# A decoder layer on one core: the work ahead of the loop over the tiles of heads in another order

## The chip, the core and the metric

The kernel runs on one core of a Trainium2 chip. A core has five engines, each with its own list of instructions and no scheduler between them: TensorE (PE) multiplies, with its weight loads shown apart (PEld), VectorE (DVE), ScalarE (ACT) and GpSimd (POOL) work on vectors, and SyncE (SP) issues the transfers. They wait for each other only where the program says so, with semaphores. The metric is the device time of one execution in microseconds (us). Before the change it is 1687.86 us, the median of 3 runs (1687.23 to 1689.83).

## The reference

One decoder layer over 8 sequences of 128 tokens, 512 features. Its first part is a Mamba-2 layer, and the change lies in the beginning of that part:

```python
proj = jnp.einsum('bsd,ed->bse', x, in_proj_w)
gate, hBC, dt = proj[..., :INTER], proj[..., INTER:INTER + CONV_DIM], proj[..., INTER + CONV_DIM:]
xc = conv_general_dilated(xc, conv_w, ...)           # 4 taps along the sequence, per channel
hBC = jax.nn.silu(xc + conv_b)                       # heads (8192 channels), B and C (8 groups of 128)
dt = jnp.clip(jax.nn.softplus(dt + dt_bias), 0.0, 100.0)
A_cum = jnp.cumsum(dt * -jnp.exp(A_log), axis=-1)    # along the sequence, 128 heads
L = jnp.exp(_segsum(A_dt))
Y_diag = jnp.einsum('bzlhn,bzshn,bhzls,bzshp->bzlhp', C, B, L, hs * dt)
g = (Y + hs * D) * jax.nn.silu(gate)                 # then a norm over each group, times out_proj_w
```

A cross attention and a gated feed-forward follow, with layer norms between; the change does not touch them.

## The kernel before

**Precision by splitting.** Every fp32 product of the projections is made of three products of rounded parts: x and the weights are split into a high part (a cast) and a low part (the difference), and `mm3` adds high x high, high x low and low x high. A projection of one tile of 128 channels over one half of the tokens (512) is 4 x 3 = 12 products of 128x512 into one PSUM bank.

**Steps.** The channels are walked in 72 steps (`STEPS`), 9 for each of 8 groups. The first step of a group projects its B (into `ps_hs`) and C (into `ps_gate`); the other 8 project one tile of heads (`heads`) and its gate (`gates`). TensorE works one step ahead: in step s it projects step s + 1, then turns and multiplies for step s. After a projection ScalarE writes the first tap with the bias (`first_tap`, into `conv`), VectorE adds the other three (`taps`, semaphore `tap`), ScalarE takes the SiLU (`silu`; `gate` for the gate's). A tile then goes: TensorE turns it to tokens (`transposes`), VectorE scales it by dt (`scale_dt`, which also frees the gate's bank), ScalarE takes four exponentials of the differences of cumulative sums (`decay`), VectorE multiplies each by the products of B and C kept in `cb`, and TensorE multiplies (`outputs`). VectorE's `taps` of the next step stand between its four decay products.

**Buffers for the weights.** `w_raw`, `w_hi` and `w_lo` have two slots, slot s % 2 for step s. GpSimd's `split(s)` makes both parts. It waits for the transfer and for the gate products of step s - 2, which read the same slot (`gate_ps` at 2s - 2).

**Cumulative sums.** dt of all heads is projected first of all into `ps_y` (weights in half of slot 1), goes through ScalarE and VectorE as softplus, is multiplied by -exp(A_log) and summed along each sequence by 8 scans. The sums go out to DRAM and come back broadcast to all partitions (`cum_load`, into `cum_bc`), where GpSimd masks what is not causal (`keep_causal`) and adds the negated sum of the other token (`differences`). TensorE turns dt and the sums to tokens (`turn_all`), and they are copied to `dt_tok` and, negated, to `neg_cum`. Both dt arrays and x share memory: `dt_v`, `dt_u`, `dt_w`, `dt_l` are the four parts of `x_raw`, named `g_acc` in the profile.

**Order.** Each engine's order is the order of the code in its block. Before the loop GpSimd makes the splits of steps 0 and 1 and both masks of tile 0; in the loop's first step it makes the split of step 2 and then both differences of tile 0. VectorE runs dt's whole chain with the scans ahead of the taps of B and C. The taps of one step are counted on one semaphore, 3 for each bank.

## Time and profile before

| what | before |
|---|---|
| time, median of 3 | 1687.86 us |
| the profiled execution's own time | 1687.67 us |
| its span | 1685.9 us |
| mean granted TensorE clock | 0.989 |
| TensorE busy | 1625.2 us, 96% of the span |
| VectorE, ScalarE, GpSimd busy | 1179.1, 948.9, 947.3 us |

The span is the time from the first to the last instruction that the profiler recorded. Busy times add up the recorded lengths; a product's recorded length holds its pipeline, so neighbouring products overlap and their pitch is less than their length. A granted clock of 1.00 is 2.4 GHz, one of 0.50 is 1.2 GHz. All rows of a timeline carry the start in us from the start of the span, the time, the engine, the line, what is written from what, and the count; a bracket names how long the engine was idle before and what ended that.

### The profile page before, as it was taken

The numbers are of one execution on the slowest core, as the hardware profiler recorded it, in microseconds if no ns is written. First come the engines' busy times: TensorE is split into PE (matmuls) and PEld (weight loads), VectorE is DVE, ScalarE is ACT, GpSimd is POOL, SyncE is SP. The second block draws the span as 40 slices with busy tenths as digits, with TensorE's granted clock in tenths as the row PEclk, the third lists the DMA queues.
The fourth block names the chain that finished last, engine by engine and source line by source line (L and its number), as shares of the span: only waits on it lengthen the run. The fifth ranks groups of instructions, "written<-read, shape, count | busy, mean of one in ns | idle before, by whom it ended". The sixth has DMA issues, their size and how long they took to land.

```text
span 1685.9 us, 25533 instructions
## 1 busy us (share of the span) xinstructions
PE 1625.2 (96%) x9160; PEld 1278.2 (76%) x9160; DVE 1179.1 (70%) x2257; ACT 948.9 (56%) x1577; POOL 947.3 (56%) x716
## 2 busy tenths in 40 slices
PE   6899999999999999999999999999999978889998
PEld 4788888888888888888888888888888865444646
DVE  4785858685868586858684868486848668896443
ACT  3583648364837383738373847384738354995231
POOL 3594839483949294929493949395929562231000
PEclk8999999999999999999999999999999989999999
DMA  5241224131423142313231323142314181001000
GB/s 206 71 136 58 99 66 135 63 101 59 135 70 101 57 132 76 101 57 132 76 100 57 132 71 105 52 135 62 115 45 137 63 139 57 1 11 29 13 13 25
DMA packets 76546, 138.84 MB, mean 82 GB/s; under 512 B 6786, under 2 KB 13954, under 8 KB 76164
## 3 DMA queue, kind: packets, MB, share of 16 engines
q1 hardware_dynamic: 76420, 137.21, 25.9%
q8 instruction: 73, 1.20, 0.3%
q14 instruction: 53, 0.43, 0.1%
HBM read 134.55 MB, written 2.63 MB: 81 GB/s over the span
## 4 chain that ended last, share of the span: by engine, by line
PE 90%; DVE 5%; ACT 2%; issue 1%; DMA 1%; SPq 1%; POOL 0%; DVEq 0%; ACTq 0%
PE ps_hs L246 8%; PE ps_hs L248 8%; PE ps_hs L247 8%; PE ps_gate L246 8%; PE ps_gate L248 8%; PE ps_gate L247 8%; PE ps_y L1123 7%; PE ps_hs L1131 7%; PE ps_hs L1133 7%; PE ps_hs L1132 7%; PE ps_gate L1112 4%; PE ps_y L1358 3%; PE ps_hs L1320 3%; PE ps_dec L1320 3%; DVE pr L959 1%
## 5 line engine op out<-in xcount | busy, mean ns | idle before, releaser
L750 DVE SCALAR_TENSOR_TENSOR conv<-ps_hs,cw,conv 128x508 f32<-128x508 f32 (+2 forms) x432 | 320.3, 742 | 30.7 <-ACT conv L511 19.6
L378 POOL TENSOR_SCALAR_AFFINE_SELECT cum_bc<-cum_bc 128x1024 f32<-128x1024 f32 x128 | 140.1, 1095 | 238.9 <-DMA cum_bc<-cum_scratch 238.2
L388 POOL TENSOR_TENSOR cum_bc<-cum_bc,neg_cum 128x1024 f32<-128x1024 f32 x128 | 247.7, 1936 | 23.1 <-DVE neg_cum L855 12.6
L246 PE MATMUL ps_hs<-x_hi,w_hi 128*128 128x512 f32 x576 | 232.6, 404 | 7.8 <-DVE conv L750 7.8
L248 PE MATMUL ps_hs<-x_hi,w_lo 128*128 128x512 f32 x576 | 225.8, 392 | 0.0
L247 PE MATMUL ps_hs<-x_lo,w_hi 128*128 128x512 f32 x576 | 225.0, 391 | 0.0
L246 PE MATMUL ps_gate<-x_hi,w_hi 128*128 128x512 f32 x576 | 224.7, 390 | 0.0
L247 PE MATMUL ps_gate<-x_lo,w_hi 128*128 128x512 f32 x576 | 224.3, 389 | 0.0
L248 PE MATMUL ps_gate<-x_hi,w_lo 128*128 128x512 f32 x576 | 224.3, 389 | 0.0
L1131 PE MATMUL ps_hs<-wo_hi,g_hi 128*128 128x512 f32 x512 | 202.6, 396 | 8.4 <-DVE acc L924 6.4
L1133 PE MATMUL ps_hs<-wo_hi,g_lo 128*128 128x512 f32 x512 | 200.7, 392 | 0.0
L1132 PE MATMUL ps_hs<-wo_lo,g_hi 128*128 128x512 f32 x512 | 200.5, 392 | 0.0
L783 DVE TENSOR_TENSOR m_sb<-ps_dec,cb 128x512 f32<-128x512 f32 x256 | 174.3, 681 | 11.4 <-ACT ps_dec L544 11.4
L361 POOL TENSOR_TENSOR w_lo<-w_raw,w_hi 128x1024 fp32r<-128x1024 f32 (+1 forms) x73 | 175.8, 2409 | 11.0 <-ACT w_hi L481 5.3
L549 ACT ACTIVATE g_hi<-ps_y 128x512 fp32r<-128x512 f32 x128 | 75.3, 588 | 183.8 <-DVE ps_y L795 183.8
L544 ACT ACTIVATE ps_dec<-cum_bc 128x512 f32<-128x512 f32 x256 | 149.4, 600 | 35.7 <-DVE m_sb L783 34.9
L791 DVE SCALAR_TENSOR_TENSOR ps_y<-hs,d_col,ps_y 128x512 f32<-128x512 f32 x128 | 96.0, 750 | 82.2 <-PE ps_y L1123 82.1
L511 ACT ACTIVATE conv<-ps_hs,cbias,cw 128x512 f32<-128x512 f32 x144 | 112.5, 783 | 70.9 <-PE ps_hs L248 70.9
L400 POOL TENSOR_TENSOR sq_acc<-sq_acc,sq_tmp 128x512 f32<-128x512 f32 x112 | 143.2, 1297 | 15.1 <-ACT sq_tmp L552 15.1
L1123 PEld LDWEIGHTS ps_y<-m_sb,xdt 128*64 128x64 f32 x2048 | 112.1, 138 | 25.9 <-issue 25.9
L246 PEld LDWEIGHTS ps_hs<-x_hi,w_hi 128*128 128x128 f32 x576 | 108.8, 189 | 29.9 <-issue 9.4
L1123 PE MATMUL ps_y<-m_sb,xdt 128*64 128x128 f32 x2048 | 127.6, 278 | 3.3 <-DVE g_lo L802 3.3
(142 smaller groups left out, 3140.0 us busy)
## 6 DMA issues: line engine op xcount, KB each, us to landing
cum_bc<-cum_scratch SPq DMA_DIRECT2D x128, 512.0 KB, 4.2
w_raw<-w_in SPq DMA_DIRECT2D x145, 256.0 KB, 4.6
wo_raw<-w_out SPq DMA_DIRECT2D x64, 256.0 KB, 5.0
g_acc<-x_t SPq DMA_DIRECT2D x4, 512.0 KB, 6.5
acc<-x_nat SPq DMA_DIRECT2D x1, 2048.0 KB, 9.3
k_rep<-ctx_t SPq DMA_DIRECT2D x8, 256.0 KB, 11.1
out<-y_out SPq DMA_DIRECT2D x8, 256.0 KB, 2.0
wg_sb<-w_gate SPq DMA_DIRECT2D x1, 1792.0 KB, 12.4
```

The source lines that it names most:

```text
L246: eng.matmul(ps, whi, xhi, start=(k == 0), stop=False)
L247: eng.matmul(ps, whi, xlo, start=False, stop=False)
L248: return eng.matmul(ps, wlo, xhi, start=False, stop=(k == n - 1))
L361: return gp.tensor_tensor(w_lo[slot][:, subs], w_raw[slot][:, subs], w_hi[slot][:, subs].bitcast(F32), ALU.subtract)
L388: gp.tensor_tensor(part, part, start.broadcast_to([P, 2, HB, SEQ]), ALU.add).then_inc(S["bc_ok"], 1)
L544: sc.activation(ps_dec[e][:, :], cum_bc[bh][:, e, :], ACT.Exp).then_inc(S["exp_ok"], 1)
L750: v.scalar_tensor_tensor(out=dst, in0=src, scalar=cw[:, at, TAPS - 1 - n:TAPS - n], in1=dst, op0=ALU.mult, op1=ALU.add).then_inc(S["tap"], 1)
L783: v.tensor_tensor(flat(m_sb[:, q]), ps_dec[q % 2][:, :], flat(half(cb, q // 2)), ALU.mult)\
L1123: mm = pe.matmul(ps_y[bh][e * HD:(e + 1) * HD, b * SEQ:(b + 1) * SEQ], xdt[:, bh * HB + b, e * HD:(e + 1) * HD], m_sb[:, 2 * bh + e, b, :] ...
L1131: pe.matmul(ps, g_hi[:, j, cols], wo_hi[:, j, :], start=(j == 0), stop=False)
L1132: pe.matmul(ps, g_hi[:, j, cols], wo_lo[:, j, :], start=False, stop=False)
L1133: return pe.matmul(ps, g_lo[:, j, cols], wo_hi[:, j, :], start=False, stop=(j == TPH - 1))
```

## The change

- TensorE first multiplies a tile of ones by itself 14 times (`WARM`), into a bank that nobody reads then.
- ScalarE copies dt's weights ahead of x, and makes the high part of step 0's weights. VectorE makes their low part. GpSimd's first full split is that of step 1.
- dt's chain uses |v| from ScalarE in place of VectorE's maximum, so that ScalarE's exponential needs no VectorE; the logarithm comes behind the first tap of B. VectorE's operations on dt and the taps of B and C alternate, and the scans come behind all four banks of taps.
- The copies to `dt_tok` and `neg_cum` are made by ScalarE. VectorE's taps of the first tile of heads follow the scans.
- SP loads the weights of steps 2 and 3 ahead of the cumulative sums' way through DRAM; GpSimd splits steps 1, 2 and 3 ahead of the masks and differences of tile 0.
- TensorE starts the first half of the first heads' products after 3 taps instead of 6, the second after 6.

On GpSimd, from dt's weights to the second tile's first mask, before:

```order
L361 TENSOR_TENSOR w_lo1<-w_raw1,w_hi1 128x512 [waits wdt_hi]
L370 CAST w_hi0<-w_raw0 128x1024 [waits w_in0]
L361 TENSOR_TENSOR w_lo0<-w_raw0,w_hi0 128x1024 [waits w_hi_ok]
L370 CAST w_hi1<-w_raw1 128x1024 [waits ps_dt,w_in1]
L361 TENSOR_TENSOR w_lo1<-w_raw1,w_hi1 128x1024 [waits w_hi_ok]
L378 AFFINE_SELECT cum_bc0<-cum_bc0 128x1024 [waits bc_in0]
L378 AFFINE_SELECT cum_bc1<-cum_bc1 128x1024 [waits bc_in1]
L370 CAST w_hi0<-w_raw0 128x1024 [waits w_in0,gate_ps]
L361 TENSOR_TENSOR w_lo0<-w_raw0,w_hi0 128x1024 [waits w_hi_ok]
L388 TENSOR_TENSOR cum_bc0<-cum_bc0,neg_cum 128x1024 [waits causal,neg_cum_ok]
L388 TENSOR_TENSOR cum_bc1<-cum_bc1,neg_cum 128x1024 [waits causal,neg_cum_ok]
L370 CAST w_hi1<-w_raw1 128x1024 [waits w_in1,gate_ps]
```

The same place on GpSimd now:

```order
L365 TENSOR_TENSOR w_lo1<-w_raw1,w_hi1 128x512 [waits wdt_hi]
L374 CAST w_hi1<-w_raw1 128x1024 [waits w_in1,w_lo_ok,ps_dt]
L365 TENSOR_TENSOR w_lo1<-w_raw1,w_hi1 128x1024 [waits w_hi_ok]
L374 CAST w_hi0<-w_raw0 128x1024 [waits w_in0,gate_ps]
L365 TENSOR_TENSOR w_lo0<-w_raw0,w_hi0 128x1024 [waits w_hi_ok]
L374 CAST w_hi1<-w_raw1 128x1024 [waits w_in1,gate_ps]
L365 TENSOR_TENSOR w_lo1<-w_raw1,w_hi1 128x1024 [waits w_hi_ok]
L382 AFFINE_SELECT cum_bc0<-cum_bc0 128x1024 [waits bc_in0]
L392 TENSOR_TENSOR cum_bc0<-cum_bc0,neg_cum 128x1024 [waits causal,neg_cum_ok]
L382 AFFINE_SELECT cum_bc1<-cum_bc1 128x1024 [waits bc_in1]
L392 TENSOR_TENSOR cum_bc1<-cum_bc1,neg_cum 128x1024 [waits causal,neg_cum_ok]
```

The split of step 0 has left GpSimd, and the split of step 3 (the last cast on `w_hi1`, which waits for gate products) has moved from behind the differences to ahead of both masks.

On VectorE, the end of dt's chain and the first taps of B (`ps_hs` 0 and 1 are the two halves of the tokens), before:

```order
L728 TENSOR_SCALAR g_acc<-g_acc 128x1024 [waits dt_dve]
L731 TENSOR_SCALAR a_col<-a_col 128x1 [waits a_exp,dt_dve]
L733 TENSOR_SCALAR g_acc<-g_acc,a_col 128x1024 [waits dt_dve]
L738 SCALAR_TENSOR_TENSOR g_acc<-ones,g_acc 128x128 [waits ones_ok,dt_dve]
L738 SCALAR_TENSOR_TENSOR g_acc<-ones,g_acc 128x128 x7
L750 SCALAR_TENSOR_TENSOR conv0<-ps_hs0,cw,conv0 128x4x127 [waits c_ok]
L750 SCALAR_TENSOR_TENSOR conv0<-ps_hs0,cw,conv0 128x4x126 [waits tap]
L750 SCALAR_TENSOR_TENSOR conv0<-ps_hs0,cw,conv0 128x4x125 [waits tap]
L750 SCALAR_TENSOR_TENSOR conv1<-ps_hs1,cw,conv1 128x4x127 [waits c_ok]
```

The same place on VectorE now, from the low part of step 0's weights on:

```order
L739 TENSOR_TENSOR w_lo0<-w_raw0,w_hi0 128x1024 [waits w_hi_ok]
L809 TENSOR_SCALAR g_acc<-g_acc 128x1024 [waits dt_act]
L811 SCALAR_TENSOR_TENSOR g_acc<-g_acc 128x1024 [waits dt_dve]
L751 SCALAR_TENSOR_TENSOR conv0<-ps_hs0,cw,conv0 128x4x127 [waits c_ok]
L751 SCALAR_TENSOR_TENSOR conv0<-ps_hs0,cw,conv0 128x4x126 [waits tap]
L751 SCALAR_TENSOR_TENSOR conv0<-ps_hs0,cw,conv0 128x4x125 [waits tap]
L816 TENSOR_TENSOR g_acc<-g_acc 128x1024 [waits dt_act,dt_dve]
L818 SCALAR_TENSOR_TENSOR g_acc<-g_acc 128x1024 [waits dt_dve]
L821 TENSOR_SCALAR g_acc<-g_acc 128x1024 [waits dt_dve]
L751 SCALAR_TENSOR_TENSOR conv1<-ps_hs1,cw,conv1 128x4x127 [waits c_ok]
```

The first three taps now stand behind two operations on dt instead of behind the whole chain and the scans.

The diff, cut to its core:

```diff
+WARM = 14
...
             sp.dma_start(acc[:, :, :], x_nat.rearrange("(b p) d -> p b d", p=P)).then_inc(S["x_in"], 16)
-            sp.wait_ge(S["dt_dve"], 16)
+            for s in range(2):
+                sp.wait_ge(S["w_lo_ok"], s + 1)
+                w_load(s + 2)
+            sp.wait_ge(S["dt_dve"], 15)
...
             for s in range(STEPS):
-                if s + 2 < STEPS:
+                if 2 <= s < STEPS - 2:
                     sp.wait_ge(S["w_lo_ok"], s + 1)
                     w_load(s + 2)
...
             pool.wait_ge(S["wdt_hi"], 1)
             w_lo_part(1, slice(0, 1)).then_inc(S["wdt_lo"], 1)
-            split(0)
+            pool.wait_ge(S["w_lo_ok"], 1)
             pool.wait_ge(S["ps_dt"], 2)
-            split(1)
-            keep_causal(0, 0)
-            keep_causal(0, 1)
+            for s in (1, 2, 3):
+                split(s)
+            for bh in range(2):
+                keep_causal(0, bh)
+                differences(0, bh)
             for s in range(STEPS):
-                if s + 2 < STEPS:
+                if 2 <= s < STEPS - 2:
                     split(s + 2)
-                if s == 0:
-                    differences(0, 0)
-                    differences(0, 1)
...
+            act.wait_ge(S["wdt_in"], 16)
+            sc.activation(w_hi[1][:, 0], w_raw[1][:, 0], ACT.Copy).then_inc(S["wdt_hi"], 1)
             for k in range(KD):
                 act.wait_ge(XT_IN[k], 16)
                 sc.activation(x_hi[:, k, :], x_raw[:, k, :], ACT.Copy).then_inc(S["x_hi_ok"], 1)
-                if k == 0:
-                    act.wait_ge(S["wdt_in"], 16)
-                    sc.activation(w_hi[1][:, 0], w_raw[1][:, 0], ACT.Copy).then_inc(S["wdt_hi"], 1)
+            act.wait_ge(W_IN[0], 32)
+            sc.activation(w_hi[0][:, :], w_raw[0][:, :], ACT.Copy).then_inc(S["w_hi_ok"], 1)
 
+            sc.activation(a_col[:, :], a_col[:, :], ACT.Exp).then_inc(S["a_exp"], 1)
             act.wait_ge(S["x_lo_ok"], KD)
             for h in range(2):
                 act.wait_ge(S["ps_dt"], h + 1)
+                sc.activation(dt_u[:, h * HALF:(h + 1) * HALF], ps_y[h][:, :], ACT.Abs, bias=dtb_col[:, :])\
+                    .then_inc(S["dt_act"], 1)
+            act.wait_ge(S["dt_act"], 2)
+            sc.activation(dt_u, dt_u, ACT.Exp, scale=-1.0).then_inc(S["dt_act"], 1)
+            for h in range(2):
                 sc.activation(dt_v[:, h * HALF:(h + 1) * HALF], ps_y[h][:, :], ACT.Identity, bias=dtb_col[:, :])\
                     .then_inc(S["dt_act"], 1)
-            sc.activation(a_col[:, :], a_col[:, :], ACT.Exp).then_inc(S["a_exp"], 1)
-            act.wait_ge(S["dt_dve"], 1)
-            sc.activation(dt_u, dt_u, ACT.Exp, scale=-1.0).then_inc(S["dt_act"], 1)
-            act.wait_ge(S["dt_dve"], 2)
-            sc.activation(dt_l, dt_w, ACT.Ln).then_inc(S["dt_act"], 1)
...
-            for sub in range(2):
-                for h in range(2):
-                    first_tap(0, sub, h)
-                for h in range(2):
-                    silu(0, sub, h)
+            first_tap(0, 0, 0)
+            act.wait_ge(S["dt_dve"], 1)
+            sc.activation(dt_l, dt_w, ACT.Ln).then_inc(S["dt_act"], 1)
+            first_tap(0, 0, 1)
+            silu(0, 0, 0)
+            first_tap(0, 1, 0)
+            silu(0, 0, 1)
+            first_tap(0, 1, 1)
+            silu(0, 1, 0)
...
+                if s == 0:
+                    first_tap(1, 0, 0)
+                    silu(0, 1, 1)
+                    first_tap(1, 0, 1)
+                    for h in range(2):
+                        act.wait_ge(S["dt_tr"], h + 1)
+                        sc.activation(half(dt_tok, h), ps_y[h][:, :].rearrange("p (b h) -> p b h", b=HB), ACT.Copy)\
+                            .then_inc(S["dt_tok_ok"], 1)
+                    silu(1, 0, 0)
+                    gate(1, 0)
+                    for h in range(2):
+                        act.wait_ge(S["cum_tr"], h + 1)
+                        sc.activation(half(neg_cum, h), ps_y[h][:, :].rearrange("p (b h) -> p b h", b=HB), ACT.Copy,
+                                      scale=-1.0).then_inc(S["neg_cum_ok"], 1)
+                    silu(1, 0, 1)
+                    gate(1, 1)
+                    continue
...
-            dve.wait_ge(S["dt_act"], 2)
-            v.scalar_tensor_tensor(out=dt_u, in0=dt_v, scalar=-1.0, in1=dt_v, op0=ALU.mult, op1=ALU.max)\
-                .then_inc(S["dt_dve"], 1)
-            dve.wait_ge(S["dt_act"], 3)
-            v.tensor_scalar(dt_w, dt_u, 1.0, None, ALU.add).then_inc(S["dt_dve"], 1)
-            dve.wait_ge(S["dt_act"], 4)
...
-            v.tensor_scalar(dt_v, dt_v, 100.0, 0.0, ALU.min, ALU.max).then_inc(S["dt_dve"], 1)
-            dve.wait_ge(S["dt_dve"], 6)
-            dve.wait_ge(S["a_exp"], 1)
-            v.tensor_scalar(a_col[:, :], a_col[:, :], -1.0, None, ALU.mult).then_inc(S["dt_dve"], 1)
-            dve.wait_ge(S["dt_dve"], 7)
-            v.tensor_scalar(dt_u, dt_v, a_col[:, 0:1], None, ALU.mult).then_inc(S["dt_dve"], 1)
-            dve.wait_ge(S["dt_dve"], 8)
-            dve.wait_ge(S["ones_ok"], 1)
-            for b in range(BATCH):
-                s0, s1 = b * SEQ, (b + 1) * SEQ
-                v.tensor_tensor_scan(dt_w[:, s0:s1], ones[:, :], dt_u[:, s0:s1], 0.0, ALU.mult, ALU.add)\
-                    .then_inc(S["dt_dve"], 1)
+            dve.wait_ge(S["w_hi_ok"], 1)
+            v.tensor_tensor(w_lo[0][:, :], w_raw[0][:, :], w_hi[0][:, :].bitcast(F32), ALU.subtract)\
+                .then_inc(S["w_lo_ok"], 1)
...
                 dve.wait_ge(S["tr_ok"], 2 * t + r + 1)
+                if t == 0:
+                    dve.wait_ge(S["dt_tok_ok"], r + 1)
...
+            dve.wait_ge(S["dt_act"], 3)
+            v.tensor_scalar(dt_w, dt_u, 1.0, None, ALU.add).then_inc(S["dt_dve"], 1)
+            dve.wait_ge(S["dt_dve"], 1)
+            v.scalar_tensor_tensor(out=dt_u, in0=dt_w, scalar=-1.0, in1=dt_u, op0=ALU.add, op1=ALU.subtract)\
+                .then_inc(S["dt_dve"], 1)
             taps(0, 0, 0)
+            dve.wait_ge(S["dt_dve"], 2)
+            dve.wait_ge(S["dt_act"], 6)
+            v.tensor_tensor(dt_l, dt_l, dt_u, ALU.subtract).then_inc(S["dt_dve"], 1)
+            dve.wait_ge(S["dt_dve"], 3)
+            v.scalar_tensor_tensor(out=dt_v, in0=dt_v, scalar=0.0, in1=dt_l, op0=ALU.max, op1=ALU.add)\
+                .then_inc(S["dt_dve"], 1)
+            dve.wait_ge(S["dt_dve"], 4)
+            v.tensor_scalar(dt_v, dt_v, 100.0, 0.0, ALU.min, ALU.max).then_inc(S["dt_dve"], 1)
             taps(0, 0, 1)
-            for h in range(2):
-                dve.wait_ge(S["dt_tr"], h + 1)
-                v.tensor_copy(half(dt_tok, h), ps_y[h][:, :].rearrange("p (b h) -> p b h", b=HB))\
-                    .then_inc(S["dt_tok_ok"], 1)
+            dve.wait_ge(S["a_exp"], 1)
+            v.tensor_scalar(a_col[:, :], a_col[:, :], -1.0, None, ALU.mult).then_inc(S["dt_dve"], 1)
+            dve.wait_ge(S["dt_dve"], 6)
+            v.tensor_scalar(dt_u, dt_v, a_col[:, 0:1], None, ALU.mult).then_inc(S["dt_dve"], 1)
             taps(0, 1, 0)
             taps(0, 1, 1)
+            dve.wait_ge(S["dt_dve"], 7)
+            dve.wait_ge(S["ones_ok"], 1)
+            for b in range(BATCH):
+                s0, s1 = b * SEQ, (b + 1) * SEQ
+                v.tensor_tensor_scan(dt_w[:, s0:s1], ones[:, :], dt_u[:, s0:s1], 0.0, ALU.mult, ALU.add)\
+                    .then_inc(S["dt_dve"], 1)
...
-                    if s == 0:
-                        for h in range(2):
-                            dve.wait_ge(S["cum_tr"], h + 1)
-                            v.tensor_scalar(half(neg_cum, h), ps_y[h][:, :].rearrange("p (b h) -> p b h", b=HB),
-                                            -1.0, None, ALU.mult).then_inc(S["neg_cum_ok"], 1)
-                        taps(s + 1, 0, 1)
...
-                pe.wait_ge(S["tap"], 3 * conv_at(s) + 6)
+                pe.wait_ge(S["tap"], 3 if s == 0 else 3 * conv_at(s) + 6)
...
+            pe.wait_ge(S["ones_ok"], 1)
+            for n in range(WARM):
+                pe.matmul(ps_dec[1][:, 0:P], ones[:, :], ones[:, :], start=True, stop=True)
...
                     heads(s + 1, 0)
+                    if s == 0:
+                        pe.wait_ge(S["tap"], 6)
                     heads(s + 1, 1)
                     if s == 0:
                         pe.wait_ge(S["ident_ok"], 1)
-                        pe.wait_ge(S["dt_act"], 4)
-                        pe.wait_ge(S["dt_dve"], 6)
+                        pe.wait_ge(S["dt_act"], 5)
+                        pe.wait_ge(S["dt_dve"], 5)
                         turn_all(dt_v, "dt_tr")
                         cb_products(s)
                     free_gate(s, 0)
                     gates(s + 1, 0)
                     if s == 0:
                         pe.wait_ge(S["dt_tok_ok"], 2)
-                        pe.wait_ge(S["dt_dve"], 16)
+                        pe.wait_ge(S["dt_dve"], 15)
                         turn_all(dt_w, "cum_tr")
                     free_gate(s, 1)
                     gates(s + 1, 1)
```

## Rows read from the trace of the kernel before

**Rows 1.** The page: the chain that ended last by engine, and one group.

```profile
PE 90%; DVE 5%; ACT 2%; issue 1%; DMA 1%; SPq 1%; POOL 0%; DVEq 0%; ACTq 0%
...
L511 ACT ACTIVATE conv<-ps_hs,cbias,cw 128x512 f32<-128x512 f32 x144 | 112.5, 783 | 70.9 <-PE ps_hs L248 70.9
```

**Rows 2.** The timeline of TensorE, 16 to 75 us.

```profile
16.12 0.50 PE L246 MATMUL ps_hs<-x_hi,w_hi 128*128 128x512 f32 x1
...
26.90 0.39 PE L248 MATMUL ps_gate<-x_hi,w_lo 128*128 128x512 f32 x1
...
35.06 0.77 PE L246 MATMUL ps_hs<-x_hi,w_hi 128*128 128x512 f32 x1 [7.77 <-DVE conv L750]
...
47.65 4.28 PE L1093 MATMUL ps_dec<-sg,hs 128*128 128x128 f32 x16 [3.81 <-ACT sg L528]
...
55.27 1.03 PE L1102 MATMUL ps_y<-ident,g_acc 128*128 128x128 f32 x8
...
60.70 1.06 PE L1112 MATMUL ps_gate<-ident,hs 128*128 128x128 f32 x8 [1.66 <-ACT sg L534]
...
72.60 1.97 PE L1123 MATMUL ps_y<-m_sb,xdt 128*64 128x128 f32 x32
74.50 1.09 PE L1112 MATMUL ps_gate<-ident,hs 128*128 128x128 f32 x8
```

**Rows 3.** Windows: length; busy us of PE, PEld, DVE, ACT, POOL; clock; DMA share; GB/s.

```profile
29.50:30.00 0.50, 0.00 (x0) 0.00 (x0) 0.50 (x3) 0.00 (x0) 0.00 (x0) 0.50 0.00 0
...
35.00:39.80 4.80, 4.74 (x11) 3.80 (x12) 0.00 (x0) 1.91 (x3) 1.64 (x2) 0.51 1.00 341
...
47.60:53.40 5.80, 5.62 (x20) 4.98 (x21) 4.24 (x7) 2.46 (x5) 0.00 (x0) 0.50 0.00 0
...
100.00:110.00 10.00, 10.00 (x73) 8.32 (x72) 8.16 (x14) 7.97 (x13) 9.76 (x8) 1.00 0.21 68
```

**Rows 4.** The timeline of VectorE, 8 to 65 us.

```profile
8.90 3.78 DVE L711 TENSOR_TENSOR x_lo<-g_acc,x_hi 128x1024 fp32r<-128x1024 f32 x3 [1.43 <-ACT x_hi L478]
...
19.59 1.68 DVE L718 TENSOR_SCALAR g_acc<-g_acc 128x1024 f32<-128x1024 f32 x1 [1.13 <-ACT g_acc L491]
...
26.18 0.69 DVE L728 TENSOR_SCALAR g_acc<-g_acc 128x1024 f32<-128x1024 f32 x1
...
27.88 2.63 DVE L738 TENSOR_TENSOR_SCAN g_acc<-ones,g_acc 128x128 f32<-128x128 f32 x8
30.43 4.48 DVE L750 SCALAR_TENSOR_TENSOR conv<-ps_hs,cw,conv 128x508 f32<-128x508 f32 x6
...
63.18 1.28 DVE L774 TENSOR_TENSOR xdt<-ps_gate,dt_tok 128x512 f32<-128x512 f32 x2
```

**Rows 5.** The timeline of GpSimd, 11 to 71 us.

```profile
11.94 1.64 POOL L370 CAST w_hi<-w_raw 128x1024 fp32r<-128x1024 f32 x1 [3.35 <-DMA w_raw<-w_in]
...
17.46 3.25 POOL L361 TENSOR_TENSOR w_lo<-w_raw,w_hi 128x1024 fp32r<-128x1024 f32 x1
37.91 1.11 POOL L378 TENSOR_SCALAR_AFFINE_SELECT cum_bc<-cum_bc 128x1024 f32<-128x1024 f32 x1 [17.20 <-DMA cum_bc<-cum_scratch]
...
40.55 1.04 POOL L370 CAST w_hi<-w_raw 128x1024 fp32r<-128x1024 f32 x1 [0.19 <-DMA w_raw<-w_in]
41.67 2.38 POOL L361 TENSOR_TENSOR w_lo<-w_raw,w_hi 128x1024 fp32r<-128x1024 f32 x1
...
67.18 1.09 POOL L378 TENSOR_SCALAR_AFFINE_SELECT cum_bc<-cum_bc 128x1024 f32<-128x1024 f32 x1 [3.25 <-DMA cum_bc<-cum_scratch]
68.36 1.92 POOL L388 TENSOR_TENSOR cum_bc<-cum_bc,neg_cum 128x1024 f32<-128x1024 f32 x1
```

**Rows 6.** The timeline of ScalarE, 10 to 62 us.

```profile
10.37 1.06 ACT L478 ACTIVATE x_hi<-g_acc 128x1024 fp32r<-128x1024 f32 x1 [0.20 <-DMA g_acc<-x_t]
...
60.57 1.28 ACT L544 ACT_TABLE_LOAD   x1
61.86 1.12 ACT L544 ACTIVATE ps_dec<-cum_bc 128x512 f32<-128x512 f32 x2
```

17 lines of the change are left out of this document (4 added, 13 removed).

## The prediction

> **What bounds the kernel now.** I read the chain that ended last first: nine tenths of it is TensorE [rows 1]. So the time is TensorE's products plus the places where TensorE has nothing to do or runs slowly. Its timeline shows where those are [rows 2]. The first projection of B and C starts at 16.12 us and its 48 products run without a hole until 27.3 (the row at 26.90 is the 48th, so 47 steps in 10.78 us, 0.229 us each; 12 products are 2.75 us, 24 are 5.5, 48 are 11.0). Then TensorE stands still for 7.8 us until 35.06, for 3.8 until 47.65 and for 1.7 until 60.70. From 60.70 on the next row of the same kind stands at 74.50, 13.8 us later, with no idle time before it: the loop over the tiles of heads runs as fast as TensorE can. The windows give the second loss [rows 3]: after 7.8 us without work the granted clock is 0.50, that is 1.2 of 2.4 GHz, and the 11 products between 35.0 and 39.8 take 0.43 us each; the products of B with C and the beginning of the next projection run at 0.50 as well.
>
> So only the stretch before 60.70 can be shortened by this change, and all that follows moves with the start of the transposes of a tile, if nothing behind it comes late. I therefore work out two moments: T1, the first transposes (60.70 before), and T2, the second (74.50 before). What is saved at T2 is saved at the end.
>
> **The start.** dt's products need the low part of x, whose fourth piece VectorE ends at 8.90 + 3.78 = 12.68 [rows 4]. The 14 products of ones and the copy of dt's weights ahead of x let TensorE begin earlier and fast, but the last six products cannot start before 12.7 and end at 14.1 (6 x 0.229). The first weights of B and C have landed at 11.94, where GpSimd's cast starts behind a DMA [rows 5]. Now ScalarE copies them behind its own last copy of x (10.37 + 1.06 = 11.43 [rows 6]): 11.94 + 1.06 = 13.0. VectorE subtracts them behind its x pieces: 3.78 / 3 = 1.26 for one of this size, 14.3. So the projection starts at 14.3 instead of 16.12: 1.8 us. If the products of ones do nothing for the clock, the last group runs at 0.43 and costs 1.2 us of that; that is one bound, and 1.8 the other.
>
> **TensorE from 14.3 on.** 48 products: 25.3. The next weights must be split: GpSimd's subtraction ended before at 17.46 + 3.25 = 20.7 at the latest [rows 5], and it starts no later now. The wait for the taps asks for three taps instead of six. VectorE's order gives them: ScalarE's chain after dt's products at 14.1 is two 128x512 reads, 0.6 us each (1.12 for two at 61.86 [rows 6]), and one exponential, 1.06, so 16.6 with some tenths for the handovers; plus one, 1.68 beside a busy GpSimd as at 19.59, or 0.69 as at 26.18 [rows 4]; I take 1.68, as GpSimd splits then. One more of 1.26: 19.5. Three taps are half of the row of six, 4.48 / 2 = 2.24: 21.8, before 25.3. ScalarE's logarithm, with its table load of 1.28 [rows 6] and its 1.06, is done by about 21 and lies beside these taps. Then 1.26 + 1.26 + 0.69 = 3.2 for dt: 25.0; three taps, 27.2, before the second half of the heads' products, 28.0; 1.0 for the negation and the product with A (26.18 + 0.69 to 27.88): 28.2; six taps: 32.7; eight scans, 2.63: 35.3. So TensorE runs on: 24 products of the first tile's heads until 30.8, the 8 transposes of dt (1.0 by the row at 55.27), 31.8, and the products of B with C. Those took 4.28 in all with a wait between and at 0.50 of the clock; I take half, 2.1, since TensorE comes without a hole: 33.9. They need the last SiLU of C at 32.7 + 0.6, and that half of them is due at 32.9: a wait of 0.4, which I leave in the roundings. 12 gate products, 36.7; the transposes of the cumulative sums (35.3, so 1.4 us to spare), 37.7; 12 more, 40.4. ScalarE's last SiLU and gate: VectorE's six taps of the tile end at 35.3 + 4.5 = 39.8, SiLU at 40.4, and the gate, which waits for the products' end, at 41.1. T1 is then 41.2 instead of 60.70: 19.5 us saved. In terms: 1.8 from the start, 7.8 and 3.8 of waits, 1.0 of the third, 2.2 for eleven products at half clock, 2.1 in B with C, 0.8 for the four slow gate products.
>
> **What the moves add.** GpSimd's order now has the splits of steps 2 and 3 ahead of the causal masks and the differences of the first tile. That of step 3 writes the weight buffer that the gate products of step 1 read, so it waits for their end, 40.4 here. Queued behind it on GpSimd are the mask and the difference of both halves, and ScalarE's exponentials wait for those, VectorE's products with them, and TensorE's outputs. Before, the first mask started at 37.91 and the differences ran beside the gate products, so that the first exponential could start at 61.86. Prices: a split from 40.55 to 41.67 + 2.38 = 44.05, 3.5 us; a mask and a difference from 67.18 to 68.36 + 1.92 = 70.28, 3.1 us [rows 5]. So 43.9, 47.0 and 50.1. The first exponential starts at 47.0, and dt's scaling of x, which frees the bank of the gate, ends 2.6 us after it (61.86 [rows 6] to 63.18 + 1.28 [rows 4]): 49.7. TensorE has done transposes (1.0) and 24 products since 41.2 and is there at 47.7: a new wait of 2.0. 24 gate products: 55.2; first half of the outputs, (74.50 - 72.60) / 2 = 0.95: 56.1. The other half waits for the last decay: third exponential 50.1 to 50.7, first tap 0.8 [rows 1], 51.5, three taps 53.7, a product of about 0.64 (half of the 1.28 for two), three taps, a product: 57.2. A second wait of 1.1, and T2 is 58.2 instead of 74.50. 3.2 of the 19.5 are given back; 16.3 remain. That GpSimd costs nothing is the lower bound of this term. The upper is 6.6, all that lies between the end of the gate products and the first difference.
>
> Does it stay? The next tile's broadcasts start when the exponentials have read their buffers, about 48.1 and 52.1, and before they were on GpSimd 4.2 us after that (the mask at 67.18 after the two exponentials from 61.86 to 62.98), so GpSimd is done with them at 55.4 and 59.4. The first is wanted at T2, 58.2, the second by the third exponential, some 2 us later (two exponentials, a decay). They are in time, narrowly.
>
> **Other moves at no cost.** The weights of steps 2 and 3 go out on SP ahead of the cumulative sums. SP waits there for two splits, 20.7 at the latest, and the sums are not ready before 35.3; the transfers hide behind 25.3 and 40.4, when their splits can start anyway. The sums' own way to GpSimd was 37.91 - (27.88 + 2.63) = 7.4 us [rows 4, 5], so 42.7, within the 43.9. If that cover goes, each us beyond adds one. Copying dt and the negated sums on ScalarE costs four times 0.6 between 33 and 39, where it waited before.
>
> ScalarE's rows say that a table load takes 1.28 us and that the next activation follows at once (60.57 + 1.28 = 61.85, next at 61.86 [rows 6]). The Trainium skill, "ScalarE: Activation LUTs", section "What ACT_TABLE_LOAD costs", speaks against threading the logarithm between taps: 1.28 us and then about 1.38 of drain, some 2.66 for every switch. By that the logarithm would be 1.4 later, dt about 0.6 later, and the sum would be some 15.7 saved instead of 16.3. The trace does not show the drain, and the row decides.
>
> **Rivals.** (a) GpSimd's bill is not felt. For it: the outputs, which need the differences in the end, started 13.6 us behind the gate products (60.70 - 1.66 to 72.60). Against it: the scaling of x stands behind the first decay on VectorE. It gives 19.5 saved. (b) The clock falls in the new wait. TensorE ended at 27.3 and at 29.50 to 30.00 the clock was 0.50 already, so 2.2 us were enough; 1.7 before 60.70 were not, and the new wait is 2.0. Then about 4.8 us run at half (as from 35.0 to 39.8), 2.4 lost, of which 1.1 falls into the wait behind: 15.0 saved. Products of ones that do not warm the clock, so that this part of the change does not do what it says, give nearly the same, 15.1. (c) The interleaved chain comes late or GpSimd keeps its lag through the first group: from 100 to 110 us it was busy 9.76 of 10 [rows 3], so it cannot make good there what it has missed. I price it at 2 us more, the same size as the first new wait, which would then come once again: 14.3 saved. (d) The other sign: with the masks late, GpSimd and not TensorE sets the pace of all the inner steps. 56 tiles are not the first of their group; from 16.3 / 56 = 0.29 us a step on, the kernel is slower, and at 0.35 it ends 3.3 us above. Against it: the first step of every group has no masks and differences on GpSimd, so a lag from the prologue cannot live on.
>
> **Numbers.** The sum is made against the profiled execution: 1687.67 (span 1685.9), 0.2 below the median of 1687.86. Forecast, 0.58: 1687.67 - 16.3 + 0.2 = 1671.6. (a) 0.10: 1668.4. (b) 0.15: 1672.9. (c) 0.12: 1673.6. (d) 0.05: around 1688 to 1691, of which I give 0.02 to within 0.2% (3.4 us, about what a measurement of this kernel can tell from none) and 0.03 to slower. Faster is the rest, 0.95. The bounds of the start (1.2) and of GpSimd's term (0 to 6.6, I take the working's 3.2) reach from 1668.4 to 1676.2; the range is 1667.0 to 1675.5.
>
> **What would show it.** Right: the projection of B and C starts near 14.3; TensorE's rows have no idle time above 0.5 us from there to 40, with the clock at 1.00; transposes near 41.2; GpSimd's first mask near 44, and behind it waits of TensorE of about 2 and 1 us ended by VectorE; second transposes near 58, then steps of 13.8. Wrong: a wait between 25 and 40, a mask before 41, a clock of 0.50 after 47, or any step in the loop longer than before. The first would leave the interleaved chain as the bound, the last would bring (d).

## The result, and the profile after

The changed kernel took 1675.87 us in the median (1674.20, 1674.78, 1676.96, 1677.26), the kernel before 1688.54 on the same chip: a ratio of 0.9925, 95% interval 0.9907 to 0.9942. 12.7 us are saved where 16.3 were forecast, and the time is 0.4 us above the range. The kernel before was 0.7 us slower here than in the runs that the forecast started from (1687.86), so it is the 3.6 us of saving that have to be explained, not the 0.4. The profiled execution took 1674.20, with a span of 1672.5.

TensorE's timeline after, first the stretch that [rows 2] show of before (start us, us, engine, line, operation, tiles, shapes, count, and in brackets the idle time before and what ended it). T1 is the start of the transposes of the first tile of heads, T2 that of the second. The profile counts 28 rows for the 14 products of ones:

```profile
1.20 5.16 PE L1162 MATMUL ps_dec<-ones 128*128 128x128 f32 x28 [1.20 <-POOL ones L359]
...
13.46 0.39 PE L247 MATMUL ps_hs<-x_hi,w_hi 128*128 128x512 f32 x1
...
31.70 1.16 PE L1110 MATMUL ps_dec<-sg,hs 128*128 128x128 f32 x8 [0.70 <-ACT sg L533]
33.91 1.16 PE L1110 MATMUL ps_dec<-sg,hs 128*128 128x128 f32 x8 [1.05 <-ACT sg L533]
42.22 0.95 PE L1129 MATMUL ps_gate<-ident,hs 128*128 128x128 f32 x7 [0.78 <-ACT sg L539]
50.84 0.50 PE L247 MATMUL ps_gate<-x_hi,w_hi 128*128 128x512 f32 x1 [2.08 <-DVE xdt L777]
58.39 1.09 PE L1140 MATMUL ps_y<-m_sb,xdt 128*64 128x128 f32 x16 [0.79 <-DVE m_sb L786]
59.70 1.07 PE L1129 MATMUL ps_gate<-ident,hs 128*128 128x128 f32 x8 [0.22 <-ACT sg L539]
```

The projection of B and C starts at 13.46, the first transposes (T1) at 42.22 and the second (T2) at 59.70, against 16.12, 60.70 and 74.50 in [rows 2]. The waits of 7.8 and 3.8 us are gone. Two waits of 0.70 and 1.05 stand before the two halves of the products of B with C, and three of 2.08, 0.79 and 0.22 between T1 and T2. At T2 14.8 us are saved, but only 13.5 at the end (13.4 of the span).

Why B with C waits is on VectorE, here after, where [rows 4] showed the chain of before (same columns):

```profile
11.95 1.23 DVE L739 TENSOR_TENSOR w_lo<-w_raw,w_hi 128x1024 fp32r<-128x1024 f32 x1
15.48 2.77 DVE L809 TENSOR_SCALAR g_acc<-g_acc 128x1024 f32<-128x1024 f32 x1 [2.31 <-ACT g_acc L495]
...
21.64 1.22 DVE L816 TENSOR_TENSOR g_acc<-g_acc 128x1024 f32<-128x1024 f32 x1
...
24.77 2.29 DVE L751 SCALAR_TENSOR_TENSOR conv<-ps_hs,cw,conv 128x508 f32<-128x508 f32 x3
26.97 0.14 DVE L824 TENSOR_SCALAR a_col<-a_col 128x1 f32<-128x1 f32 x1
27.15 1.63 DVE L826 TENSOR_SCALAR g_acc<-g_acc,a_col 128x1024 f32<-128x1024 f32 x1
```

and GpSimd's splits and masks beside it, which answer to [rows 5]:

```profile
15.30 2.40 POOL L365 TENSOR_TENSOR w_lo<-w_raw,w_hi 128x1024 fp32r<-128x1024 f32 x1
...
25.82 2.41 POOL L365 TENSOR_TENSOR w_lo<-w_raw,w_hi 128x1024 fp32r<-128x1024 f32 x1
41.51 1.04 POOL L374 CAST w_hi<-w_raw 128x1024 fp32r<-128x1024 f32 x1 [13.28 <-PE ps_gate L249]
42.63 2.40 POOL L365 TENSOR_TENSOR w_lo<-w_raw,w_hi 128x1024 fp32r<-128x1024 f32 x1
44.98 1.10 POOL L382 TENSOR_SCALAR_AFFINE_SELECT cum_bc<-cum_bc 128x1024 f32<-128x1024 f32 x1
```

The "plus one" of dt's chain (L809) takes 2.77 us, from 15.48 to 18.25, while GpSimd subtracts from 15.30 to 17.70. The product with A (L826) takes 1.63 while GpSimd subtracts from 25.82. Three taps, which read PSUM, take 2.29 partly beside GpSimd's subtraction (24.77) and 2.29 without it (19.43). And the first mask starts at 44.98, behind step 3's split, as the forecast had it (43.9, with T1 1.0 earlier).

The other difference lies 1,300 us later, behind the last tile of heads. The changed kernel there:

```profile
1367.48 3.54 PE L1156 MATMUL ps_y<-ones,sq_acc 128*128 128x1 f32 x16 [2.69 <-POOL sq_acc L404]
...
1375.34 1.06 DVE L950 TENSOR_SCALAR mask_sb<-mask_sb 128x128 f32<-128x128 f32 x1 [4.01 <-DMA mask_sb<-attn_mask]
1376.29 2.48 POOL L464 TENSOR_TENSOR k_bd<-k_rep,kbd_mask 128x512 f32<-128x512 f32 x2
1376.55 2.77 DVE L763 SCALAR_TENSOR_TENSOR acc<-g_acc,rstd_g,acc 128x512 f32<-128x512 f32 x2
...
1380.03 0.80 PE L1148 MATMUL ps_hs<-wo_hi,g_hi 128*128 128x512 f32 x1 [6.24 <-DVE acc L941]
1380.63 0.63 PE L1149 MATMUL ps_hs<-wo_lo,g_hi 128*128 128x512 f32 x1
```

and VectorE's same rows in the kernel before:

```profile
1388.41 0.80 DVE L933 TENSOR_SCALAR mask_sb<-mask_sb 128x128 f32<-128x128 f32 x1 [3.97 <-DMA mask_sb<-attn_mask]
1389.13 0.19 DVE L768 RECIPROCAL rstd_g<-rstd_g 128x8 f32<-128x8 f32 x1
1389.36 2.76 DVE L762 SCALAR_TENSOR_TENSOR acc<-g_acc,rstd_g,acc 128x512 f32<-128x512 f32 x2
```

The attention mask is scaled on VectorE, and queued behind it are the updates of `acc` for which TensorE waits. The scaling waits for a transfer. I count from the last tile's transposes (1367.18 before, 1352.42 after): it starts 21.2 us behind them before and 22.9 after, and the rest of the program ends 318.7 and 320.1 behind them. That is the 1.4 us between 14.8 and 13.4.

### The profile page after: what moved, and what is told of

It is laid out like the page before. It is cut to its first block, busy times and chain, and to the rows that moved or that the text cites. A ratio compares the mean times of both kernels' runs of the same rounds, so it can differ in the third digit from the quotient of the medians.

```text
span 1672.5 us, 25592 instructions
## 1 busy us (share of the span) xinstructions
PE 1625.8 (97%) x9188; PEld 1280.1 (77%) x9188; DVE 1177.8 (70%) x2253; ACT 953.0 (57%) x1584; POOL 940.9 (56%) x714
## 4 chain that ended last, share of the span: by engine, by line
PE 89%; DVE 5%; ACT 2%; issue 1%; DMA 1%; SPq 1%; POOL 0%; DVEq 0%; POOLq 0%; ACTq 0%
PE ps_hs L247 8%; PE ps_hs L249 8%; PE ps_hs L248 7%; PE ps_gate L247 7%; PE ps_gate L248 7%; PE ps_gate L249 7%; PE ps_hs L1148 7%; PE ps_y L1140 7%; PE ps_hs L1149 7%; PE ps_hs L1150 7%; PE ps_gate L1129 4%; PE ps_y L1380 3%; PE ps_hs L1342 3%; PE ps_dec L1342 3%; DVE pr L976 1%
## 5 line engine op out<-in xcount | busy, mean ns | idle before, releaser
L751 DVE SCALAR_TENSOR_TENSOR conv<-ps_hs,cw,conv 128x508 f32<-128x508 f32 (+2 forms) x432 | 320.3, 742 | 30.4 <-ACT conv L516 19.2
L786 DVE TENSOR_TENSOR m_sb<-ps_dec,cb 128x512 f32<-128x512 f32 x256 | 174.3, 681 | 16.2 <-ACT ps_dec L549 16.2
L365 POOL TENSOR_TENSOR w_lo<-w_raw,w_hi 128x1024 fp32r<-128x1024 f32 (+1 forms) x72 | 172.1, 2390 | 8.5 <-ACT w_hi L480 2.8
L404 POOL TENSOR_TENSOR sq_acc<-sq_acc,sq_tmp 128x512 f32<-128x512 f32 x112 | 143.3, 1297 | 14.9 <-ACT sq_tmp L557 14.9
L435 POOL CAST wo_hi<-wo_sc 128x512 fp32r<-128x512 f32 x64 | 39.1, 611 | 158.8 <-PE ps_hs L1150 158.7
```

What stands on the lines that cost most here:

```text
L365: return gp.tensor_tensor(w_lo[slot][:, subs], w_raw[slot][:, subs], w_hi[slot][:, subs].bitcast(F32), ALU.subtract)
L751: v.scalar_tensor_tensor(out=dst, in0=src, scalar=cw[:, at, TAPS - 1 - n:TAPS - n], in1=dst, op0=ALU.mult, op1=ALU.add).then_inc(S["tap"], 1)
L786: v.tensor_tensor(flat(m_sb[:, q]), ps_dec[q % 2][:, :], flat(half(cb, q // 2)), ALU.mult)\
```

## The experiments

One table for all. "Start" is the start of the projection of B and C; T1 is counted from it, T2 from T1; "mask" is the start of the mask's scaling and "tail" the end of the span, both counted from the last tile's transposes; "fall" is where the granted clock fell to 0.50 (1.2 of 2.4 GHz) between the start and T2, for 3.4 us unless said otherwise. These are of the profiled execution; the median is of all.

| kernel | start | T1 | T2 | mask | tail | fall | median | ratio to before (95%) |
|---|---|---|---|---|---|---|---|---|
| before | 16.1 | 44.6 | 13.8 | 21.2 | 318.7 | 29.5 (10.2), 46.6 (6.8) | 1688.5 | |
| changed | 13.5 | 28.8 | 17.5 | 22.9 | 320.1 | none | 1675.9 | .9925 (.9907-.9942) |
| e1 same again | 14.4 | 30.2 | 17.5 | 25.0 | 321.6 | 35.2 | 1676.1 | .9921 (.9907-.9934) |
| e2 split behind add | 13.9 | 27.3 | 17.5 | 24.4 | 319.8 | none | 1673.0 | .9904 (.9889-.9919) |
| e3 masks first | 13.8 | 28.7 | 15.3 | 23.4 | 320.9 | none | 1673.0 | .9902 (.9889-.9916) |
| e4 no products of ones | 17.5 | 28.6 | 17.5 | 24.5 | 320.3 | none | 1677.4 | .9928 (.9915-.9940) |
| e5 = e2 + e3 | 13.6 | 27.3 | 15.4 | 21.5 | 318.2 | none | 1671.4 | .9885 (.9870-.9900) |
| e6 waits filled | 14.6 | 28.6 | 17.8 | 25.1 | 321.4 | 52.0 | 1675.8 | .9908 (.9894-.9921) |
| e7 six taps | 14.5 | 30.5 | 17.5 | 25.0 | 320.9 | 29.0 | 1676.6 | .9910 (.9896-.9923) |
| e8 loads late | 13.7 | 27.5 | 25.6 | 25.9 | 321.8 | 44.5 (6.8), 58.1 | 1682.3 | .9942 (.9930-.9955) |
| e9 step 0 on GpSimd | 15.3 | 30.4 | 17.5 | 21.2 | 316.8 | 36.2 | 1678.5 | .9935 (.9922-.9949) |
| e10 mask load first | 13.4 | 30.3 | 17.5 | 18.4 | 310.6 | 34.0 | 1666.0 | .9867 (.9853-.9880) |
| e11 before + that | 16.8 | 43.6 | 13.8 | 17.1 | 312.4 | 32.3, 45.9 (both 6.8) | 1682.2 | .9963 (.9949-.9977) |
| e12 = e5 + e10 | 14.0 | 27.3 | 15.6 | 17.3 | 309.2 | none | 1661.1 | .9837 (.9824-.9851) |
| e13 = e2 + e10 | 14.2 | 27.3 | 17.8 | 16.5 | 308.3 | 50.4 | 1663.8 | .9845 (.9830-.9859) |
| e14 = e3 + e10 | 13.7 | 28.7 | 15.2 | 17.4 | 309.5 | none | 1664.2 | .9842 (.9828-.9855) |
| e15 = e6 + e10 | 14.9 | 28.7 | 17.8 | 18.5 | 312.3 | 52.7 | 1665.3 | .9852 (.9838-.9866) |
| e16 = e12 + one wait filled | 14.4 | 27.4 | 15.1 | 18.5 | 310.6 | none | 1661.0 | .9826 (.9813-.9840) |

**e1, the changed kernel again.**

> The changed kernel once more, unaltered, for its spread and for where its slower executions lose. The profiled execution saved 14.8 us at the second transposes but 13.5 at the end, and the timed executions lay at 1674.2, 1674.8, 1677.0 and 1677.3. Theory: the stretch up to the end of the last tile repeats within 0.3 us, the last 300 us differ by up to 3 us from execution to execution because the clock falls at other moments of the idle places there; times spread over 1674 to 1677.5, and where this profile's time is above 1676 its second transposes still stand at 59.7 and its loss lies behind 1360 us. Rival: the slower executions lose at the new wait of 2.1 us near 49 us, where the clock falls; then the second transposes stand 1.5 to 3 us later (61 to 63) in such a profile, with a granted clock of 0.50 behind 49.

1676.06. Both expectations were half right. A fall came in this execution, but behind the waits before B with C, not behind the wait of 2.08. The windows of e1 (stretch; its length, then busy time and count of PE, PEld, DVE, ACT, POOL; granted clock, DMA share, GB/s):

```profile
31.80:35.20 3.40, 1.66 (x12) 1.47 (x13) 3.33 (x8) 2.55 (x4) 0.00 (x0) 1.00 0.00 0
35.20:38.60 3.40, 3.40 (x12) 2.91 (x12) 3.33 (x8) 1.24 (x3) 0.00 (x0) 0.50 0.37 151
38.60:42.00 3.40, 3.40 (x20) 2.84 (x19) 3.33 (x6) 2.37 (x5) 0.00 (x0) 0.99 0.48 131
```

It costs 1.5 us (T1 30.2 instead of 28.8 behind the start). So one kernel has executions with and without it. The tail differs too (321.6 and 320.1), as the theory had it; what sets it comes at e10.

**e2, GpSimd's splits behind VectorE's chain.**

```diff
-            for s in (1, 2, 3):
-                split(s)
+            pool.wait_ge(S["dt_dve"], 2)
+            split(1)
+            pool.wait_ge(S["dt_dve"], 7)
+            split(2)
+            split(3)
```

> GpSimd's split of step 1 waits until VectorE has made its first two operations on dt, and its split of step 2 until VectorE has multiplied dt by A. Nothing else differs from the changed kernel. Theory: VectorE's addition (2.77 us) and multiplication (1.63 us) on 128x1024 were stretched because GpSimd worked on SBUF beside them; alone they take 0.7 and 0.75, VectorE's chain is 2 us earlier at the taps of C, TensorE's two waits before the products of B with C (0.7 and 1.05 us) fall to under 0.3 together, and the first transposes stand at 40.5 to 40.9 instead of 42.2; the time falls by 1.3 to 1.7 us. Rival: the addition is long for another reason (ScalarE reading and writing the same tile's memory); then it stays above 2 us and the transposes at 42.2. Second rival: the split of step 1 becomes late and TensorE waits at 24.3 for it; then the transposes stand later than 42.2.

VectorE's rows in e2:

```profile
15.92 0.69 DVE L812 TENSOR_SCALAR g_acc<-g_acc 128x1024 f32<-128x1024 f32 x1 [2.37 <-ACT g_acc L498]
...
20.19 2.54 DVE L819 TENSOR_TENSOR g_acc<-g_acc 128x1024 f32<-128x1024 f32 x1
...
27.02 0.75 DVE L829 TENSOR_SCALAR g_acc<-g_acc,a_col 128x1024 f32<-128x1024 f32 x1
```

The add takes 0.69 and the product 0.75. Now the subtraction pays: it lies beside the moved split (19.25 to 21.65) and takes 2.54, where the changed kernel has 1.22. So it is GpSimd's subtraction that stretches what VectorE does on SBUF at that moment, in three different places now, while it takes its own 2.40 in all of them; ScalarE's work on the same memory, the rival, is the same in e2. How much is lost can be read from the rows. While both run, VectorE hardly moves: 2.08 us lost in 2.22 shared at 15.48, 1.32 in 1.46 at 20.19 of e2, 0.88 in 1.08 at 27.15. It is the one that started first that keeps its pace. In the kernel before, VectorE started first once:

```profile
16.90 1.56 DVE L715 SCALAR_TENSOR_TENSOR g_acc<-g_acc 128x1024 f32<-128x1024 f32 x1 [4.22 <-ACT g_acc L487]
```

and there GpSimd's subtraction, which started at 17.46, took 3.25 instead of 2.40 [rows 5]. (VectorE's own 1.56 instead of 1.23 began beside a cast of GpSimd's that had started at 16.34.)

The second wait before B with C is gone and T1 is 1.4 us nearer to the start. The first wait stayed at 0.74, which I had not expected, so T1 is at 41.2 and not at 40.5 to 40.9; the median of 1673.0 is 3.0 below e1's, more than the 1.3 to 1.7 expected, with overlapping intervals. The Trainium skill, "GPSIMD Engine Reference", section "1. Specifications", says that GpSimd shares its SBUF interfaces with VectorE, with contention for VectorE's instructions in a two-port mode or with two SBUF inputs. The trace agrees for these rows (2.77, 2.54 and 1.63 against 0.69, 1.22 and 0.75), and with the taps, whose one input is in PSUM, at 2.29 either way.

**e3, the masks ahead of step 3's split.**

```diff
-            for s in (1, 2, 3):
-                split(s)
+            split(1)
+            split(2)
             for bh in range(2):
                 keep_causal(0, bh)
                 differences(0, bh)
+            split(3)
```

> GpSimd makes the split of step 3 behind the masks and differences of tile 0 instead of ahead of them; the rest is the changed kernel. Theory: the split's 3.5 us and its wait for the gate products are what makes the first exponential late (48.2). Without them the first mask starts when the sums have landed (42 to 43.5), the first exponential near 46, TensorE's waits of 2.1 and 0.8 us behind fall to under 0.5 together, and the second transposes stand at 56.8 to 57.3 instead of 59.7; the time falls by 2.4 to 2.9 us. Rival: the sums' transfer is the real bound behind the split, landing just before the masks; then the first mask starts at 44.5 or later and the gain is under 0.7. Second rival: the split of step 3 becomes late for its products and takes the gain back at the third tile.

GpSimd in e3:

```profile
43.10 1.10 POOL L382 TENSOR_SCALAR_AFFINE_SELECT cum_bc<-cum_bc 128x1024 f32<-128x1024 f32 x1 [14.62 <-DMA cum_bc<-cum_scratch]
```

The mask now waits for the transfer of the sums and not for the split. The wait of 2.08 is gone, that of 0.79 stays, and T2 is 15.3 behind T1 instead of 17.5 (at 57.8, where 56.8 to 57.3 were expected). Step 3's split, 49.33 to 52.85, is not missed: the next steps keep their 13.8.

**e4, without the products of ones.**

> The 14 products of ones are left out; the rest is the changed kernel. Theory: dt's products begin at 7.7 at half clock (0.43 us apart), the clock rises after about 4 to 5 us, the projection of B and C starts 1.5 to 2.5 us later (15 to 16), and since TensorE waits 1.75 us before the products of B with C anyway, the first transposes move by 0.5 to 1 us only: time up by 0.5 to 1.5 us. Rival: the products of ones are what carries all of the earlier start; then the transposes move by the whole 2 us or more.

The clock rose only at 15.9 and the start was at 17.5: 3 to 4 us later than in its neighbours, not the 1.2 that I had priced, and T1 moved with it: by the profile the rival is right. The median is only 1.3 above that of e1, with overlapping intervals; what made up the difference between profile and median I can't say.

**e5, e2 and e3 together.**

> Both changes of GpSimd together: splits of steps 1 and 2 behind VectorE's operations on dt, and the split of step 3 behind tile 0's masks. Theory: the first saves 1.0 us at the first transposes (41.2 instead of 42.2), the second 1.9 at the second (57.8 instead of 59.7), and they only partly add, because the masks then wait for the sums' transfer (landed at 43.1 with the scans ending at 36.0; the scans now end at 34.7, so 42.0): second transposes at 56.6 to 57.2, time 1 to 1.5 us under either alone, about 1672 (median of the two alone 1673.0). Rival: the scans are not earlier, the transfer binds alone: second transposes at 57.6 to 57.9 and the time of the masks alone.

T2 came 18.2 us earlier than before, at 56.3 where 56.6 to 57.2 were expected: the two edits add.

**e6, products of ones in the waits before B with C** (3 ahead of the first half, 4 ahead of the second).

> The changed kernel with 3 products of ones ahead of the first half and 4 ahead of the second half of the products of B with C, into a bank that is written afterwards; they fill the two waits of 0.7 and 1.05 us there. The computation is unchanged. Theory: in the slower profile of the changed kernel the clock stood at 0.50 from 35.2 to 38.6, right behind these waits, and its second transposes were 2.4 us later than in the fast one; with the waits filled the clock does not fall there, no profile has its second transposes later than 60.5, and the times keep to 1674 to 1676 (median 1674.5 to 1675.3 against 1676.1). Rival: the fall comes from elsewhere or is taken at random; the times spread as before (up to 1678) and the median stays within 0.5 us of 1676. Second rival: the filling products delay the real ones; the second transposes stand 0.3 to 0.8 us later.

```profile
50.00:52.00 2.00, 0.13 (x1) 0.13 (x2) 2.00 (x4) 0.34 (x1) 1.85 (x2) 1.00 0.24 74
52.00:55.40 3.40, 3.40 (x9) 2.62 (x10) 2.08 (x4) 2.49 (x4) 1.61 (x3) 0.51 0.36 121
```

No fall between 30 and 45, but one at 52.0, behind the wait of 2.08: rival (b) of the forecast exists. It costs only 0.3 us (T2 17.8 instead of 17.5 behind T1): the waits of 0.79 and 0.22 behind it are gone. The median can't be told from that of e1.

**e7, six taps before step 1's first product instead of three.**

```diff
-                pe.wait_ge(S["tap"], 3 if s == 0 else 3 * conv_at(s) + 6)
+                pe.wait_ge(S["tap"], 3 * conv_at(s) + 6)
```

> TensorE waits for six taps again before the first half of the first heads' products; the rest is the changed kernel. Theory: it then starts them at 27.1 instead of 24.3, ends them at 32.7 instead of 30.0, and since it waits 1.75 us before the products of B with C anyway (until 31.7 and 33.9), the second part of the delay is absorbed: transposes of dt to 33.6, products of B with C end at 35.8 instead of 34.8; the transposes of tile 0 stand 0.9 to 1.2 us later (43.1 to 43.4) and the time is up by about 1 us. A wait of 2.7 us may let the clock fall and add up to 1.7. Rival: no cover, the whole 2.7 us is lost at the first transposes.

A wait of 2.3 ends at 27.9 and the two before B with C vanish into it. T1 is 1.7 later; the eight products at half clock behind the fall at 29.0 make 1.5 of it. The median is within the interval of e1's.

**e8, the loads of steps 2 and 3 where they were before.**

```diff
-            for s in range(2):
-                sp.wait_ge(S["w_lo_ok"], s + 1)
-                w_load(s + 2)
...
-                if 2 <= s < STEPS - 2:
+                if s + 2 < STEPS:
```

> SP loads the weights of steps 2 and 3 behind the cumulative sums again, as in the kernel before; the rest is the changed kernel. Theory: the load of step 2 goes out at 39.5 and lands at 43 to 44.5, its split on GpSimd ends at 47 to 48, the split of step 3 at 50.5 to 51.5; TensorE's heads' products of step 2 start at 47 to 48 instead of 43.0 (a wait of 4 to 5 us, long enough for the clock to fall), and the masks, behind both splits, make the first exponential start at 54 to 55 instead of 48.2. The second transposes stand 5.5 to 7.5 us later than 59.7 and the time is up by as much. Rival: the load hides anyway behind the masks' lateness and the time is up by under 2 us.

TensorE in e8:

```profile
48.40 0.79 PE L247 MATMUL ps_hs<-x_hi,w_hi 128*128 128x512 f32 x1 [6.17 <-POOL w_lo L362]
```

The moved loads, which the forecast had "at no cost", are worth about 7 us at T2, as expected: they are a condition of the gain. There is a second thing to see in this run. Step 2's split comes late, so GpSimd stands idle beside the product with A, but not beside the "plus one":

```profile
15.67 2.38 DVE L806 TENSOR_SCALAR g_acc<-g_acc 128x1024 f32<-128x1024 f32 x1 [2.21 <-ACT g_acc L492]
...
26.94 0.75 DVE L823 TENSOR_SCALAR g_acc<-g_acc,a_col 128x1024 f32<-128x1024 f32 x1
```

T1 is 27.5 behind the start all the same, against 27.3 in e2 and 28.8 in the changed kernel. So most of what e2 gains at T1 is the product with A.

**e9, step 0's weights split by GpSimd.**

> The changed kernel with step 0's weights split by GpSimd again (cast and subtraction, in front of its other splits) instead of by ScalarE and VectorE. Theory (the split on two engines opens the way to the first product of the B and C projection): w_raw lands at about 10.9, GpSimd needs 4.3 us for a pair of tiles in one stretch where ScalarE and VectorE together take some 2.5, so the projection starts at 15.0 to 15.6 instead of 13.5 to 14.4, a wait of 1 to 1.5 opens behind the products of dt, first transposes of a tile 1 to 1.5 later than in the unaltered changed kernel (43.2 to 44.5 against 42.2), second 60.7 to 61.5, time 1 to 1.5 us above the changed kernel. Rival (the load of x, not the split, sets the start): projection at 13.5 to 14.4 as before, nothing lost.

The start is at 15.29, behind a wait of 1.49 ended by GpSimd's subtraction. The term is right: 1 to 2 us by the start. The median is 2.4 above e1's, and so it is by the ratios, with overlapping intervals, where 1 to 1.5 were expected.

**e10, the changed kernel with the load of `attn_mask` ahead of `k_rep`.** One line of SyncE's row moved:

```diff
             sp.wait_ge(S["gate_ps"], 2 * STEPS)
+            sp.dma_start(mask_sb[:, :], attn_mask).then_inc(S["m3_in"], 16)
             for par in range(2):
...
             sp.dma_start(v_raw[:, :, :], ctx_nat.rearrange("b t d -> t b d")).then_inc(S["v_in"], 16)
-            sp.dma_start(mask_sb[:, :], attn_mask).then_inc(S["m3_in"], 16)
```

> The changed kernel, with the load of attn_mask put in front of the eight of k_rep in SyncE's row, and nothing else. In ten profiled executions so far the stretch from the last tile's transposes to the end took 318.2 to 321.6 us, and in each the scaling of that mask on VectorE stands ahead of the last updates of acc and waits for the transfer, which lands 21.1 to 25.1 after those transposes behind 2.5 MB of other loads. Theory (this landing, not the clock, sets the length of the tail): VectorE's first update of acc starts right behind the square sums, at about 19.5 after the transposes instead of 24, the tail is 315 to 316.5, and the time 1671 to 1673 (4 to 5 below the changed kernel, ratio near .989 to .990), whatever the clock does there. Rival (the products of the tail at half clock set it): the tail stays at 319.5 to 321.5 and the time at 1675 to 1677.

```profile
1372.23 0.22 DVE L950 TENSOR_SCALAR mask_sb<-mask_sb 128x128 f32<-128x128 f32 x1
...
1372.90 1.42 DVE L763 SCALAR_TENSOR_TENSOR acc<-g_acc,rstd_g,acc 128x512 f32<-128x512 f32 x2
...
1375.03 0.69 PE L1148 MATMUL ps_hs<-wo_hi,g_hi 128*128 128x512 f32 x1 [0.25 <-DVE acc L941]
1375.56 0.39 PE L1149 MATMUL ps_hs<-wo_lo,g_hi 128*128 128x512 f32 x1
```

1666.01, with all runs between 1665.7 and 1666.9: 10 us less than the changed kernel (9 by the ratios, the two being from different sets of runs), twice what I expected. The first update of `acc` starts 19.1 instead of 24.1 behind the last transposes, as expected. What I had missed: the pair of updates now takes 1.42 instead of 2.77, since GpSimd's `k_bd` (2.48 for two at 1376.29) no longer runs beside it, and TensorE's wait of 6.24 is 0.25. The tail is 9.5 us shorter, and the rows say where. 6.4 are gained when that product of TensorE starts (21.2 instead of 27.6 behind the last transposes). 1.4 more come with the next nine products, which in the changed kernel run at half clock behind the long wait (rows of 0.63, granted clock 0.50 from 1377.1 to 1383.9) and here at full clock (rows of 0.39). The last 1.5 are a fall of the clock at 1510.2 in the changed kernel's profile, in the attention, which e10's doesn't have. The clock still fell twice ahead of the updates (at 1361.8 and 1368.6, for 3.4 and 6.8 us) and the gain came all the same. So the landing is the larger part of it, the clock the smaller, and one of its falls comes from the landing's wait.

**e11, the kernel before with the same move.**

> The kernel before with that one load moved in the same way. Theory: its tail of 318.7 falls to 314 to 316, its time by 3 to 4.5 us (ratio .9975 to .998), and against the changed kernel with the same move the difference is what is saved at the second transposes, 13 to 15 us. Rival (the tail of the kernel before is shorter since its clock falls later): tail still 318 to 319, ratio 1.000.

1682.24, 6.6 us less (ratio .9963). Against e10 the change is now worth 16.2 in the medians and 14.9 in the profiles, 13.1 of them at T2. The tail is 1.8 shorter in e10 than in e11; 1.5 of that arise where the clock falls once more in e11 and not in e10 (window of e11, same columns as before):

```profile
1517.00:1521.00 4.00, 4.00 (x23) 2.68 (x21) 2.35 (x6) 2.22 (x6) 1.60 (x3) 0.57 0.27 77
```

**e12, e5 with the mask load first.**

> The best version so far (GpSimd's split of step 1 behind VectorE's second operation of dt's chain, of step 2 behind its later subtraction, and of step 3 behind the masks of the first tile) with the load of attn_mask ahead of k_rep. Theory: the gains add, since they lie in other stretches: first transposes 40.9 to 41.5, second 56.3 to 57.5, tail 315 to 316.5, time 1664 to 1669, ratio near .9855 to .987. Rival: as e5 (ratio .9885), the tail's length being that of the clock.

1661.07: the gains add, and both e5 and e10 are beaten.

**e13 to e16: the terms ahead of the loop once more, with the tail's scatter taken out.**

> e10 (mask load ahead of k_rep) with e2's edit: GpSimd splits steps 1 to 3 only behind VectorE's add and subtraction of dt's chain. Theory: the late add is what opened the second wait before the products of B with C, and with it the fall of the clock behind it: first transposes 27.3 behind the start instead of 28.7 or 30.3, no fall of the clock between 30 and 45, time 1.4 to 3 us below e10's 1666.0 (1663 to 1664.6, ratio .985 to .986 against .9867). Rival (only the 1.4 us of waiting count, the clock's fall is filled by later waits): 1.0 to 1.4 below; other rival (all of it runs into the wait for the product of x with dt): 0.

> e10 with e3's edit: the masks and differences of the first tile ahead of step 3's split on GpSimd. Theory (the forecast's term for GpSimd, 3.2, of which 2.1 was the wait for the scaling of x): second transposes 15.4 behind the first instead of 17.5, time 2 to 2.4 below e10 (1663.6 to 1664). Rival (GpSimd's later split comes late for step 3): T2 gains 2 but the loop gives it back, 1666.

> e10 with e6's edit: 3 and 4 products of ones ahead of the two waits before the products of B with C. Theory (the clock's falls behind these waits cost up to 1.6 us, in about half of the executions, the waits themselves stay as work): no fall between 30 and 45; the median 0 to 1 below e10 (1665 to 1666). Rival (the fall is put off to the wait of 2.1 at 48, as it was at 52.0 in e6): as e10 or up to 1 above.

> e12 (all moves of GpSimd's order and the mask load) with 3 products of ones in the one wait of 0.7 that is left before the products of B with C. Theory: that wait is too short to let the clock fall, so nothing is won: as e12, ratio .983 to .9845. Rival (the clock's falls decide): 1 to 2 below e12.

Against e10 (1666.0, from another set of runs; the intervals reach 2.4 us to each side) e13 is at 1663.8, e14 at 1664.2, e15 at 1665.3. e13 and e14 are where their theories put them, but a difference of 2 us is within these intervals; their profiles are what tells it: T1 27.3 behind the start in e13, T2 15.2 behind T1 in e14. The expectation that the clock does not fall between 30 and 45 came in for both e13 and e15. e15 can't be told from e10, and its profile shows the fall put off to 52.7, as in e6. e16 equals e12 (1661.0), so nothing is won by filling the one wait of 0.7 that is left. These two are the best versions.

## Why the prediction was wrong

**Right.** The start: 14.3 forecast, 13.4 to 14.9 in the kernels that keep the split of step 0 on two engines and the products of ones; e9 and e4 show that both are needed. The waits of 7.8 and 3.8 are gone. GpSimd's bill of 3.2, as waits of 2.0 and 1.1: they are 2.08 and 0.79, and e3 removes the first by the order alone. That refutes rival (a). Rival (c) with its lag and rival (d) are refuted too: steps behind T2 keep their 13.8, and the saving at T2 (14.80) stands at 14.76 at the last tile.

**Wrong, first step: the wait before B with C, "a wait of 0.4, which I leave in the roundings".** The sum held nothing for it, and it is 0.70 and 1.05. This is the first thing that the forecast had named as a sign of being wrong, a wait between 25 and 40. T1 is at 42.2 instead of 41.2, though the projection starts 0.8 earlier than forecast: 28.8 behind it instead of 26.9, and of the 1.9 between, 1.75 are the two waits. What ends last there is VectorE's chain. It began 1.1 earlier than forecast (15.48 instead of 16.6), and the "plus one", 2.77 where I had 1.68 from a row of before, took just that back: the first taps start at 19.43, forecast 19.5. Then comes the product with A, 1.63 where I had 0.69, beside a split of GpSimd's for which the working had not looked there: the first taps of C start at 28.70 instead of 28.2. So of the 1.0 by which T1 is late in absolute time, 0.5 are this price and 0.4 are the wait that I had seen and not added. e2 and e8 take the split away from the product, and T1 comes 1.4 and 1.3 nearer to the start; e13 did as e2. T2 lies another 0.5 further behind T1 than forecast, 0.3 of it at the very end, where TensorE waits 0.22 for ScalarE's gate, a wait that the working didn't have. Together that is 1.5 us of the profile's miss.

In three of the seven profiled kernels that have both waits (changed, e1, e3, e4, e9, e10, e14) the clock fell behind them, for 1.5 to 1.6 us more (e1, e9, e10), in none of the five that have only the first (e2, e5, e8, e12, e13; e16 fills it). That the median of the changed kernel lies 1.7 above its profiled execution fits this, but no run shows the clock of an execution that wasn't profiled. The forecast had written that a wait of 1.7 leaves the clock alone; here two that sum to 1.75, 1.16 us of products between them, did not always.

**Wrong, second step: "what is saved at T2 is saved at the end".** 14.8 was saved at T2 and 13.5 at the end. The stretch behind the last tile hangs on a transfer. Over the 11 profiled kernels that load the mask last, its scaling starts 21.2 to 25.9 us behind the last transposes, and the tail is 316.8 to 321.8 long: the three early ones (21.2, 21.5, 21.2) have the three shortest tails (316.8, 318.2, 318.7), the latest the longest. The change touches nothing there. The profile of before that I worked from was an execution with an early landing, and the changed one's was in the middle: this part of the miss is the luck of two executions, and the forecast's error is to have taken one execution's tail for the kernel's. e10 and e11 took the transfer out of the way and 10 and 6.6 us went. Whether the kernel before lands early more often than the changed one is not shown: it has one profile with the mask last, and that the move gains 3 us less in it leaves the question open. In e11 the last large load (`v_raw`) landed 24.0 behind the last transposes, later than in e10 (22.6), which speaks against it. My first reading of this stretch had been the clock, which falls there too, in other places in each execution. e6 spoke against it: its square sums ran at nearly full clock (2.08 us instead of 3.54) and its tail was still 321.4. e10 then showed that the clock has a share all the same, 2.9 of the 9.5 us there.

Together: 1.5 and 1.4 make the 2.9 between 16.3 and the 13.4 by which the profiled span is shorter. The other 0.7 of the 3.6 by the medians is that the changed kernel's median lies 1.7 above its profiled execution and that of before 0.9; what those executions lost, no run shows. The bounds that the forecast worked out reached to 1676.2, and only the range was cut to 1675.5; but the two terms from which those bounds came are not the ones that failed.

## What to carry to other kernels

Before "the saving stays to the end" is written down, look for the first place behind the change where an engine's row waits for a transfer, and see in two executions whether it lands at the same distance; in such a place the order of a load of 64 KB and 2.5 MB was worth 10 and 6.6 us, where the whole change was worth 12.7. A price of VectorE on SBUF is only good together with what GpSimd does at the same moment: in this kernel the one that starts second loses nearly all the time that the two share, so lay both timelines side by side for every operation of the chain, not for one. GpSimd's subtraction beside taps that read PSUM cost nothing. When work moves ahead on one engine, name who is queued behind it: here masks behind a split that could end 7.8 us later without being missed (52.85 in e3 instead of 45.03).

## What the runs showed of the hardware

- Beside GpSimd's two-input subtraction (2.40 us) VectorE's one-input operation of 128x1024 on SBUF took 1.63 to 2.77 instead of 0.69 or 0.75, and its two-input one 2.54 instead of 1.22: 0.81 to 0.94 of the shared time was lost where GpSimd started first. Where VectorE started first (before, 16.90), the subtraction took 3.25. Taps that read PSUM didn't change (2.29 for three).
- ScalarE's table load shows 1.28 and the next activation follows 0.01 later (17.29, then 18.58 in the changed kernel), as the forecast had read it from [rows 6].
- The granted clock can fall to 0.50 for 3.4 us behind waits as short as 2.08 (e6, e13, e15; 2.10 in e8) or 0.7 and 1.05 close together (e1, e9, e10), and in other executions of the same kernel it doesn't.
- The eight loads of `k_rep` (256 KB each) landed 11.3 us after their issue in one execution and 13.3 in another (medians of the eight, e5 and e6), and the mask, queued behind them, 21.4 and 25.1 us behind the last transposes.
